# Gate rows of a two-layer graph network: upper part and bias added by accumulating DMAs instead of by VectorE and GpSimd

## The reference

```python
u = rgcn(x)                                  # messages summed per node, plus x @ root + bias
z = concatenate([u, x], 1) @ w_gate + b_gate # the gate
h = tanh(u) * z + x * (1 - z)
x = layernorm(x + h)                         # X1, read by the second layer
msg = (x @ W)[src] * norm                    # second layer: H = X1 @ W, then a sum over edges
x = layernorm(x + relu(segment_sum(msg) + b))
```

## Time and profile before

| | us |
|---|---|
| median of 3 runs | 1625.65 (1625.63 to 1625.74) |
| span of the profiled execution | 1624.1 |
| time around that span, by the median | 1.55 |
| PE busy in the span | 1597.2 |
| upper gate products (line 886) | from 1266 to 1331 |
| tail (lines 952, 979) | from 1331 to 1523 |
| last part (line 1045 on) | from 1523 to 1624 |

### The profile page before, as it was taken

The page is one execution under the profiler, slowest core; times in us unless marked ns, Lnnn a source line. Parts: engine busy times, 40 slices in busy tenths (PEclk is TensorE's granted clock), DMA queues, the critical chain, the costliest instruction groups (busy, mean ns, idle before and its releaser), DMA issues.

```text
span 1624.1 us, 23696 instructions
## 1 busy us (share of the span) xinstructions
PE 1597.2 (98%) x7947; PEld 1308.5 (81%) x7947; DVE 1127.3 (69%) x1894; ACT 575.9 (35%) x963; POOL 838.1 (52%) x823
## 2 busy tenths in 40 slices
PE   8999999999999999999999999999999998999997
PEld 7888888888877777788888888888888876888886
DVE  4856655655457667748878785778788869767486
ACT  4211111111133434425655553555555652222000
POOL 1000777777766666537777772777676601222000
PEclk9999999999999999999999999999999999999999
DMA  6322444444322121267777874777778785666643
GB/s 236 103 87 81 129 115 131 112 108 141 83 79 79 59 78 64 67 229 226 247 234 219 250 222 143 236 238 228 231 227 279 273 292 171 238 215 225 267 145 117
DMA packets 122124, 280.34 MB, mean 173 GB/s; under 512 B 23143, under 2 KB 24407, under 8 KB 121873
## 3 DMA queue, kind: packets, MB, share of 16 engines
q0 software_dynamic: 38256, 104.17, 22.3%
q1 hardware_dynamic: 46912, 98.19, 18.8%
q10 hardware_dynamic: 36832, 76.44, 12.5%
HBM read 209.97 MB, written 83.10 MB: 180 GB/s over the span
## 4 chain that ended last, share of the span: by engine, by line
PE 93%; DVE 3%; DMA 2%; issue 1%; ACT 0%; POOL 0%; SPq 0%; ACTq 0%; DVEq 0%; POOLq 0%
PE PG L790 67%; PE PG L979 6%; PE PG L1045 5%; PE PM L802 3%; PE PG L886 3%; PE PM L813 3%; PE PM L814 3%; PE PG L952 2%; DMA y<-STAGE 1%; PE PM L848 1%; PE PM L831 1%; PE PM L772 0%; DMA WRAW<-in_L_gnn_weight_dram 0%; PE PM L961 0%; DMA XROWS<-in_x_dram 0%
## 5 line engine op out<-in xcount | busy, mean ns | idle before, releaser
L790 PE MATMUL PG<-WHI,XHI 128*128 128x512 f32 x1600 | 631.7, 395 | 2.2 <-DVE WLO L1310 2.2
L790 PE MATMUL PG<-WHI,XLO 128*128 128x512 f32 x1600 | 623.5, 390 | 0.0
L790 PE MATMUL PG<-WLO,XHI 128*128 128x512 f32 x1600 | 623.0, 389 | 0.0
L790 PEld LDWEIGHTS PG<-WHI,XHI 128*128 128x128 f32 x1600 | 300.9, 188 | 64.5 <-issue 2.5
L790 PEld LDWEIGHTS PG<-WHI,XLO 128*128 128x128 f32 x1600 | 300.6, 188 | 63.7
L790 PEld LDWEIGHTS PG<-WLO,XHI 128*128 128x128 f32 x1600 | 301.0, 188 | 60.0
L1095 ACT ACTIVATE STAGE<-PG 128x512 f32<-128x512 f32 x200 | 119.1, 596 | 452.8 <-PE PG L790 452.6
L1310 DVE TENSOR_TENSOR WLO<-WRAW,WHI 128x512 fp32r<-128x512 f32 x176 | 122.1, 694 | 223.4 <-ACT WHI L1088 223.1
L711 POOL DMA_INDIRECT WORK<-y,REC x184 | 202.7, 1102 | 91.7 <-issue 49.3
L658 POOL DMA_INDIRECT records<-RREC,IDX x160 | 210.1, 1313 | 61.0 <-issue 43.7
L711 POOL DMA_INDIRECT RAW<-y,REC x184 | 204.2, 1110 | 70.4 <-issue 48.0
(11 more groups left out here) (265 smaller groups left out, 2257.3 us busy)
## 6 DMA issues: line engine op xcount, KB each, us to landing
y<-STAGE ACTq DMA_DIRECT2D x220, 256.0 KB
WRAW<-in_L_gnn_weight_dram SPq DMA_DIRECT2D x128, 256.0 KB, 3.2
EDGE_ROWS<-edge_rows POOLq DMA_DIRECT2D x10, 1000.0 KB, 6.2
WRAW<-in_L_gnn_w_gate_dram SPq DMA_DIRECT2D x32, 256.0 KB, 4.2
WORK<-y SPq DMA_DIRECT2D x15, 512.0 KB, 4.4
WORK<-x SPq DMA_DIRECT2D x10, 512.0 KB, 4.7
WORK<-in_x_dram SPq DMA_DIRECT2D x9, 512.0 KB, 3.7
XROWS<-in_x_dram SPq DMA_DIRECT2D x9, 512.0 KB
```

Of the source, the lines that this page charges most:

```text
L790: last = pe.matmul(PG[:, bank, :], lhs[:, k, t * P:(t + 1) * P], rhs[:, j % 2, k, :], start=(k == 0 and n == 0), stop=(k == KT - 1 and n = ...
```

## The change

The upper rows no longer go through a tile of their own. POOL adds them to GATE[t % 2] by a DMA with `accum_op=add`, waits until it has landed (`upper_added`), and adds the bias by a second accumulating DMA, whose source is b_gate repeated for all 128 partitions. That DMA's end is `gate_set`, for which `make_z(t)` now waits at every t. `gate_bias` and the additions of POOL are gone, with the tiles GATE_UPPER and BIAS_GATE and the load of the latter. SP's `load_gate` loads the gate rows alone. Further, `upper_bank(n)` becomes 1 + (n + 1) % 3, so that bank 1 is last used by n = 17, and `gate(0, 1)`, which writes bank 1, waits for 18 copies of ACT where it waited for 20; the waits at n = 0, 1, 2 follow the banks.

```diff
         def upper_bank(n):
-            return 1 + n % 3
+            return 1 + (n + 1) % 3
...
             def load_gate(t):
                 if t == 0:
                     sp.wait_ge(pair_done, 2 * NPAIR)
+                    for b in range(2):
+                        sp.wait_ge(y_out[b], 16 * (UNITS_Y + 4) * NT // 2)
                 if t == 1:
                     sp.wait_ge(u_ready, 2)
-                    sp.wait_ge(u0_turned, NT)
-                if t == 2:
-                    sp.wait_ge(upper_done, 2 * NT)
-                for b in range(2):
-                    sp.wait_ge(y_out[b], 16 * ((UNITS_Y + 4) * NT // 2 + t + 1))
                 after(sp, mixed, t - 1)
-                for rows, part in ((GATE[t % 2].rearrange("p (h n) -> p h n", h=2), gate_d), (gate_upper_of(t), upper_d)):
-                    sp.dma_start(rows, part[bass.ds(t * P, P), :, :]).then_inc(gate_in[t % 2], 16)
+                sp.dma_start(GATE[t % 2].rearrange("p (h n) -> p h n", h=2), gate_d[bass.ds(t * P, P), :, :]).then_inc(gate_in[t % 2], 16)
...
             sp.wait_ge(u0_summed, NT)
-            sp.dma_start(BIAS_GATE[:, :], b_gate.partition_broadcast(P)).then_inc(bias_gate_in, 16)
             load_gate(0)
...
+            def gate_sum(t):
+
+                gate = GATE[t % 2]
+                pool.wait_ge(gate_in[t % 2], 16 * (t // 2 + 1))
+                for b in range(2):
+                    pool.wait_ge(y_out[b], 16 * ((UNITS_Y + 4) * NT // 2 + t + 1))
+                pool.dma_start(gate.rearrange("p (h n) -> p h n", h=2), upper_d[t * P:(t + 1) * P, :, :],
+                               accum_op=ALU.add).then_inc(upper_added, 16)
+                pool.wait_ge(upper_added, 16 * (t + 1))
+                pool.dma_start(gate, b_gate.partition_broadcast(P), accum_op=ALU.add).then_inc(gate_set, 16)
+
             pool.wait_ge(u0_summed, NT)
-            pool.wait_ge(gate_in[0], 32)
+            pool.wait_ge(gate_in[0], 16)
             load_gcn(0, 0)
             load_gcn(0, 1)
+            gate_sum(0)
             pool.wait_ge(upper_done, 2 * NT)
             load_gcn(1, 1)
+            gate_sum(1)
             pool.wait_ge(gcn_split[0], KT)
             load_gcn(1, 0)
-
-            def gate_sum(t):
-
-                gate = GATE[t % 2]
-                pool.wait_ge(gate_in[t % 2], t // 2 * 32 + 32)
-                link(nc.gpsimd.tensor_tensor(gate, gate, GATE_UPPER[:, t % 2, :], ALU.add))
-                nc.gpsimd.tensor_tensor(gate, gate, BIAS_GATE[:, :], ALU.add).then_inc(gate_set, 1)
...
-            rstd(0)
-            rstd(1)
-            for t in range(3, NT):
-                gate_sum(t)
-                rstd(t - 1)
-            for t in range(NT - 1, 2 * NT):
+            for t in range(NT - 2):
+                rstd(t)
+                gate_sum(t + 2)
+            for t in range(NT - 2, 2 * NT):
                 rstd(t)
...
                 if n < 3:
-                    pe.wait_ge(evac_done, (UNITS_Y + 4) * NT - 2 + n)
+                    pe.wait_ge(evac_done, (UNITS_Y + 4) * NT - (1, 0, 2)[n])
...
-                        pe.wait_ge(upper_taken, 2 * NT)
+                        pe.wait_ge(upper_taken, 2 * NT - (2 if t == 0 else 0))
...
-            def gate_bias(t):
-                gate = GATE[t % 2]
-                dve.wait_ge(gate_in[t % 2], t // 2 * 32 + 32)
-                if t == 0:
-                    dve.wait_ge(bias_gate_in, 16)
-                halves = gate.rearrange("p (h n) -> p h n", h=2)
-                link(V.tensor_tensor(halves, halves, gate_upper_of(t), ALU.add))
-                link(V.tensor_tensor(gate, gate, BIAS_GATE[:, :], ALU.add))
-
             def make_z(t):
 
                 bank, gate = z_bank(t), GATE[t % 2]
-                after(dve, gate_set, t - 2)
+                dve.wait_ge(gate_set, 16 * (t + 1))
                 dve.wait_ge(z_done, t + 1)
```

More of the change, by code:

```diff
@@ L173, in gnn_resnorm_kernel @@
         sp0_hi, sp0_lo = SPHI[:, 0:D], SPLO[:, 0:D]
-        BIAS_GATE = place("BIAS_GATE", [P, D], F32, "xt_lo")
-        GATE_UPPER = place("GATE_UPPER", [P, 2, D], F32, "w_hi")
         BIAS_GCN = place("BIAS_GCN", [P, D], F32, "xt_hi", 4 * NPAD * 4)
@@ L363, in gnn_resnorm_kernel @@
         upper_taken = sem("upper_taken")
+        upper_added = sem("upper_added")
         gate_set = sem("gate_set")
         bias_in = sem("bias_in")
-        bias_gate_in = sem("bias_gate_in")
         sums0_in = sem("sums0_in")
@@ L426, in row_slot @@
             return x_part[:, 2 * (t - KT):2 * (t - KT) + 2, KT * P:NPAD]
[L428 to L432, removed]
         def gcn_raw_of(h, ks):
@@ L507, in load_gate_slice @@
                 sp.dma_start(wraw[:, b, s, :], w_gate[k * P:(k + 1) * P, h * HW:(h + 1) * HW]).then_inc(w_in[b][s], 16)
-            root_d, gate_d, upper_d = (y_d[u * NPAD:(u + 2) * NPAD, :].rearrange("(h n) c -> n h c", h=2)
-                                       for u in (UNITS_Y, UNITS_Y + 2, UNITS_Y + 4))
+            root_d, gate_d = (y_d[u * NPAD:(u + 2) * NPAD, :].rearrange("(h n) c -> n h c", h=2)
+                              for u in (UNITS_Y, UNITS_Y + 2))
             def load_root(t):
@@ L592, in _ @@
             sp.wait_ge(z_done, NT)
-            sp.wait_ge(gate_set, NT - 3)
             for s in range(KT):
@@ L726, in load_gcn @@
                                rows.rearrange("(k p) n -> p k n", p=P)).then_inc(gcn_in[2 * h + c], 16)
+            upper_d = y_d[(UNITS_Y + 4) * NPAD:(UNITS_Y + 6) * NPAD, :].rearrange("(h n) c -> n h c", h=2)
+            def gate_sum(t):
[7 more added lines that the diff above has]
+                pool.dma_start(gate, b_gate.partition_broadcast(P), accum_op=ALU.add).then_inc(gate_set, 16)
             pool.wait_ge(u0_summed, NT)
-            pool.wait_ge(gate_in[0], 32)
+            pool.wait_ge(gate_in[0], 16)
             load_gcn(0, 0)
             load_gcn(0, 1)
+            gate_sum(0)
             pool.wait_ge(upper_done, 2 * NT)
             load_gcn(1, 1)
+            gate_sum(1)
             pool.wait_ge(gcn_split[0], KT)
             load_gcn(1, 0)
-            def gate_sum(t):
-                gate = GATE[t % 2]
-                pool.wait_ge(gate_in[t % 2], t // 2 * 32 + 32)
-                link(nc.gpsimd.tensor_tensor(gate, gate, GATE_UPPER[:, t % 2, :], ALU.add))
-                nc.gpsimd.tensor_tensor(gate, gate, BIAS_GATE[:, :], ALU.add).then_inc(gate_set, 1)
             def rstd(t):
@@ L1768, in _ @@
                 gcn_low(k)
-            gate_bias(1)
             make_z(0)
@@ L1781, in _ @@
                     mix(1)
-                    gate_bias(2)
                     make_z(2)
```

1 line of the change is left out of this document (removed).

## The result

The changed kernel takes **1674.47 us** (median of 4 runs, 1670.45 to 1677.46) where the kernel before took 1625.7 in the same session (median of 4 runs, 1625.63 to 1628.75): 1.0295 times as long, 95% interval 1.028 to 1.0311. That is 41.5 us above the 1633.0 forecast and far outside the range. The profiled execution is the fastest of the four, with a span of 1668.7 us.

The account below looks back on a forecast made before the run. DVE's chain bounds the tail's entry, PE the rest; the change adds a loop of chained DMAs. Loss 15.3 less gain 7.9 is +7.4 on 1625.65, giving 1633.0 us; 8-in-10 range 1618 to 1643.

Parts of the forecast that it names:

- A: Steady tail: both accumulating DMAs of a tile from issue to landing, taken as 10.6 us; free up to 7.8, break-even 9.4.
- the upper bound: A at most 11.7 us, 5.5 + 6.2, since adding reads source and tile, 1 MB in all; net +14.0.
- 6A - 48.3: Loss in us from the loop up to make_z(8), not below zero; 15.3 at A = 10.6.
- 5.54 + 4.35 + A: One turn of the tail's loop: make_z(t) to mixed(t - 1), then gate rows and both accumulations; 20.5 us at 10.6.
- Rival 2: Adding reads twice at full price or neighbours slow it: A above 11.2, time 1637 to 1645; chance 0.23.
- rival 4: Entry: POOL waits for tile 1's first accumulation, delaying load_gcn(1, 0) past 1344; each us costs up to one; no separate chance.
- After tile 8 PE has other work to hide tile 9's sum: End of the tail: tile 9's sum was to cost PE nothing, so the loss was counted only to make_z(8).
- The gain side: Entry of the tail: DVE additions gone and slow instructions restored, conv_in(1, 0) from 1381.41 to 1374.0; 7.9 us in all.
- The bank order: Entry: gate(0, 1) runs 2.56 us earlier, but the stop moves to turn_u(2), some 3 us long; worth 0.
- The two slow DVE instructions: Entry: instructions of 2.84 and 2.87 us beside POOL's additions return to 0.8 and 0.7; 4.2 us of DVE time back.
- Tile 0's x1_ready: Entry: comes at 1349.9 instead of 1352.4; ACT's wait for load_gcn(1, 0) leaves 1.3 us of it.
- A below 8.8: Steady tail: adding costs what copying costs, net -3.4 or better, 1619.3 at 8.3; chance 0.32.

Follow-up runs that it names:

- plain_chain: Changed kernel with both accumulating DMAs made plain copies of the same bytes, shapes and waits, so gate rows are overwritten: 1646.21 us, ratio 1.0125.
- probe: Kernel before plus eight awaited single 512 KB DMAs on POOL in the last part, plain and accumulating, whole rows, halves, repeated bias: 1626.49 us in one run.
- whole_rows: Changed kernel with the upper accumulation reading contiguous 4 KB rows from other places of y instead of 2 KB halves: 1663.57 us, ratio 1.0224.
- ring_only: Changed kernel with four GATE tiles instead of two, so load_gate(t) waits for mix(t - 4), not mix(t - 2): 1625.36 us, ratio 0.9996.
- no_bias: Changed kernel without the second accumulating DMA (bias left out of the sum), one accumulation left in the loop: 1616.69 us, ratio 0.9949.
- ring_hybrid: Kernel before with the new bank order; DVE adds tiles 0 and 1, accumulating DMAs add tiles 2 to 9 in four GATE tiles: 1617.07 us, ratio 0.9941.
- ring_bias_dve: As ring_hybrid, but DVE adds the bias, leaving POOL one accumulating DMA for each tile: 1618.79 us, ratio 0.9957.
- banks_only: Kernel before with only the new turn of the upper banks and its waits: 1625.63 us, ratio 0.9997.

## Why the prediction was wrong, step by step

**Direction and mechanism held, the size did not.** The forecast stands for a span of 1631.45, and the profiled one is 1668.7, 37.2 more. The parts:

1. **A is the term that failed: 14.8 where 10.6 was taken and 11.7 was the upper bound.** With the prediction's own formula, 6A - 48.3, this is 6 x 4.2 = **25.2 us**. The formula itself was right: 5.54 + 4.35 + A gives 24.7 for the turn, measured 25.2. The bounds were drawn from plain DMAs of POOL on straight lines between sizes, 3.9 and 4.4 us for 512 KB. The tail has such landings, but only as its best: the shortest of `plain_chain` are 4.2 and 3.9, and the shortest of the changed kernel's tail 5.9 and 4.9, together 10.8. The means are 12.0 and 14.8. So adding is 2.8 of A (12.0 to 14.8), and the larger miss, some 4 us, is from the best landings to the mean ones. Rival 2 had named slow neighbours, with a chance of 0.23, but its range ended at 1645. The shapes were not priced either: in the probe 1.7 to 1.8 us hang on the upper rows' pieces of 2 KB, in the tail (`whole_rows`) 0.8 of A. The crowded median of GCNRAW, 8.3, was set aside because the DMA share in the steady tail is 0.61 on average. In the stretches in which the long ones are under way it is 0.93 and 0.91 (table by stretch above): after POOL's issue at 1401.38 ACT's store of X follows at 1401.93, SP's loads of 256 and 512 KB at 1401.96 and 1402.34, and the store of h_hi at 1403.29. That DMA took 11.0 us, and the bias behind it 4.9. For tile 3 the stores began at 1381.03, 4.1 us behind the issue at 1376.96: there the first took 5.9 and the second 7.7. So a mean share over a tile's turn was the wrong row. This reading is argued from the rows: no run took the neighbours away and left the chain as it was, and the probe's landings are long at shares of 0.73 to 0.81.
2. **The entry lost 8.1 us more than was counted.** This was rival 4, priced at up to one for one with 3 us as its example. The load of w_gcn was issued at 1348.52, not around 1343, and ACT could begin to split it 9.9 us later; 5.5 is the best landing of such a load before. Only the 5.5 us of late issue are rival 4; the landing, longer by 4.3, was in no term. Some 1.7 of the two was hidden. `mix(1)` ended at 1372.5, not at 1364.4. It came on top of the loop, as the prediction had said such a loss would. `ring_only`, where it stands alone, puts it at the whole of the gain: 1625.36 against 1617.07 of the kernel that avoids it.
3. **Other waits in the loop: 1.9 us.** `make_z(8)` came at 1517.69; 1418.85 + 6 x 14.8 + 8.1 = 1515.8. Two gaps of POOL make up most of it: tile 3's second DMA was issued 1.2 us behind the landing of the first, where 0.3 was counted, and tile 7's first one 5.0 us behind SP's issue, where 3.9 was counted. What held POOL there the rows don't show.
4. **"After tile 8 PE has other work to hide tile 9's sum" failed, for 4.6 us.** `make_z(9)` waited as well:

```profile
1542.81 0.69 DVE L1702 TENSOR_TENSOR WORK<-PG,WORK 128x512 f32<-128x512 f32 x1 [5.72 <-DMA WORK<-in_L_gnn_b_gate_dram]
```

The chain of waits goes on from there over the norm to PE's last turn and the last part without a gap:

```profile
1551.94 0.82 DVE WORK L1695
...
1552.81 1.09 PE PM L953 x8
1553.90 16.35 PE PG L971 x72
1570.25 81.61 PE PG L1037 x360
```

From `make_z(8)` to the last part it was 52.6 us, and the prediction's numbers allow 48.0 (1515.1, which is 1523.0 less the gain, less 1467.15).

5. **The end was 2.7 us shorter**, which nobody had counted: from the start of the last part to the end of the span 98.4 us against 101.1 before. See the last section.

Together 25.2 + 8.1 + 1.9 + 4.6 - 2.7 = 37.1; the last 0.1 is rounding. The median of the four runs lies 4.0 us above the profiled one's 1670.45.

**What held.** The gain side: 7.9 us were worked out, and `no_bias`, in which the loop is free, starts its last norm 8.8 us earlier (1608.35 for 1617.16); for `ring_hybrid` 5.4 follow from the same terms, and 5.3 were measured. The bank order is worth 0, and the stop moved to `turn_u(2)` with 2.96 us for the 3 forecast. The two slow DVE instructions came back to 0.81 and 0.68. Tile 0's x1_ready was worked out for 1349.9, and the norm started at 1350.27. A is free up to 7.8: at 7.5 the turn was 17.7, at 12.0 it was 22.4, at 13.9 23.9, at 14.8 25.2.

**Where the judgement went wrong.** The prediction gave a third of its chance to A below 8.8, on the ground that the plain rows had been taken beside other traffic. It did not ask what traffic its own DMAs would meet: their start is tied to `mixed`, and so are the stores and loads that ACT and SP issue right after it. And the upper end, "reads 1 MB, so costs what 1 MB costs", was no bound for the mean, since it took the best landing of 1 MB: plain copies alone already came to 12.0.

## What to carry to other kernels

When parallel loads are turned into a chain of DMAs each of which waits for the one before, write down the loop that the chain closes, through the tile that must come free, and its free time; then price each DMA by its own kind and by what will be issued beside it, not by the best row of its size: here a pair took 10.8 us at its best and 14.8 in the mean. If the loop doesn't have that time, the DMAs are not to be given up but taken out of it: two more tiles gave 49 us back here, with the landings as long as ever. And look at what a queue does behind an awaited DMA: here a load of 1 MB that PE needed stood behind tile 1's sum.

## What the runs showed of the hardware

- In the last part of `probe` an accumulating DMA of 512 KB into SBUF took 1.0 us (repeated bias) to 2.5 us (whole and split rows) more than a plain one, 7.3 to 9.3 in all. In the tail a pair cost 2.8 us more adding than plain (14.8 and 12.0), and the shortest adding landings were 5.7 (upper rows, `ring_bias_dve`) and 4.9 (bias). POOL's issue took longer in the tail too, 0.74 plain and 1.21 adding at L722, 0.57 and 0.89 at L725. In the probe it was 1.0 for both with whole rows and with the bias.
- The same accumulating DMA of the upper rows landed in 5.9 to 11.0 us within one tail (t = 2 to 9), and in 16.0 for t = 0. At the stretches shown, the shares are 0.73 for 5.9 us and 0.91 for 11.0.
- After eight of its nine stops of 2.9 to 7.9 us between 1340 and 1530 PE ran for a while at half of the full clock (matmuls 0.43 apart where it is 0.23), and eight transposes took 1.97 us where they take 1.04. The ninth is the stop of 2.98 before 1400.79: behind it the granted clock stayed at 1.00 for the whole 11.0 us of the stretch shown. Over the whole kernel PE's busy time rose by 15.8 us with the same instructions.
- The last packet of the last store, 392 KB from WORK to the output, ends 2.6 us after its issue in all ten kernels. The span ends 3.5 us after that packet in the kernel before and in `banks_only`, and 4.2 in `probe`, but 0.8 to 2.2 in all seven kernels in which the new DMAs had run in the tail. That is 1.3 to 2.7 us of their times, and it is no part of the store itself. What makes it so was not tried; it stays open.
